# A new order on all engines in the first loop of a two-layer attention and experts kernel

## What is computed

```python
x = x + conv_attention(group_norm(x))     # q.k over a 3x3 neighbourhood, softmax, v, Wo
t = tokens(x)                             # 4 images x 4096 tokens x 256
n = layer_norm(t)
g = sigmoid(tanh(n @ Wp.T + bp) @ Wg.T)   # a gate per token
t = t + windowed_sum(g * n, 64) / windowed_sum(g, 64)
n = layer_norm(t)
p, e = top_2(softmax(n @ router.T))       # 8 experts, 2 for each token
t = t + sum_over_2(p * (gelu(n @ w1[e] + b1[e]) @ w2[e] + b2[e]))
```

## Time and profile before

| | us |
|---|---|
| median of 3 runs | 1681.78 (1677.89 to 1684.32) |
| the profiled execution | 1676.88 |
| its span, first to last instruction | 1674.9 |
| busy in the span: PE, DVE, ACT, POOL | 1308.2, 1143.7, 932.6, 858.6 |
| mean granted TensorE clock | 0.878 of full speed |

### The profile page before, as it was taken

One profiled execution on the slowest core, in us unless ns is written; L12 is line 12 of the kernel. 1 busy time (PEld: TensorE's weight loads), 2 busy tenths in 40 slices (PEclk: granted clock), 3 DMA queues, 4 the chain that ended last, 5 costly groups with the idle time before them and its releaser, 6 DMA issues. The chain is left out here.

```text
span 1674.9 us, 29587 instructions
## 1 busy us (share of the span) xinstructions
PE 1308.2 (78%) x8800; PEld 1156.5 (69%) x8800; DVE 1143.7 (68%) x3961; ACT 932.6 (56%) x2027; POOL 858.6 (51%) x864
## 2 busy tenths in 40 slices
PE   2289898999989998999987259999999999623232
PEld 2178787888877787788875249999999999522222
DVE  7447888888888788888884735656565656355554
ACT  1177576676666666676753246767677776311111
POOL 2234565667657566576654506666666666500000
PEclk7599999999999999999996569999999999855555
DMA  9445522223313123132211465555455544299997
GB/s 337 140 158 111 143 73 89 83 90 99 103 64 105 67 96 108 58 105 83 86 67 54 113 164 166 167 164 170 160 169 160 171 159 159 79 340 338 328 329 271
DMA packets 117819, 248.08 MB, mean 148 GB/s; under 512 B 40481, under 2 KB 54049, under 8 KB 113441
## 3 DMA queue, kind: packets, MB, share of 16 engines
q1 hardware_dynamic: 78624, 155.71, 30.1%
q0 software_dynamic: 26112, 71.60, 12.1%
q10 hardware_dynamic: 12928, 18.89, 3.2%
HBM read 132.57 MB, written 113.57 MB: 147 GB/s over the span
## 5 line engine op out<-in xcount | busy, mean ns | idle before, releaser
L1566 POOL DMA_INDIRECT answers<-yy,dest_i x288 | 302.9, 1052 | 194.6 <-DVE dest_i L1680 123.0
L1436 POOL DMA_INDIRECT sent<-tn,slot_s x256 | 256.2, 1001 | 171.1 <-DVE mix L1289 98.8
L1692 DVE TENSOR_TENSOR xl<-m_bank,xh 128x512 fp32r<-128x512 f32 x144 | 92.9, 686 | 179.2 <-ACT xh L1662 179.1
L1788 PE MATMUL m_bank<-ident,tot 128*128 128x128 f32 x256 | 63.0, 427 | 157.6 <-DVE tot L1773 157.6
L740 PE MATMUL o_bank<-vv,at 128*128 128x256 f32 x512 | 142.4, 402 | 43.5 <-ACT at L922 23.6
L1656 ACT ACTIVATE hid<-m_bank,b1s 128x512 f32<-128x512 f32 x144 | 98.9, 689 | 134.2 <-issue 87.5
L1615 PE MATMUL s_bank<-band,hh 128*128 x576 | 167.4, 291 | 0.9 <-DVE yy L1707 0.9
L1788 PEld LDWEIGHTS m_bank<-ident,tot 128*128 128x128 f32 x256 | 50.2, 223 | 170.2 <-DVE tot L1773 170.2
L1615 PE MATMUL s_bank<-w_s,hh 128*128 x576 | 160.8, 279 | 0.0
L1615 PE MATMUL s_bank<-band,hl 128*128 x576 | 160.6, 279 | 0.0
L1802 ACT ACTIVATE fin<-m_bank 128x512 f32<-128x512 f32 x64 | 38.1, 597 | 188.2 <-PE m_bank L1788 188.2
(11 more groups left out here) (214 smaller groups left out, 3890.4 us busy)
## 6 DMA issues: line engine op xcount, KB each, us to landing
xin<-sent SPq DMA_DIRECT2D x72, 516.0 KB, 3.8
got<-answers SPq DMA_DIRECT2D x32, 1024.0 KB, 7.1
xs<-in_x SPq DMA_DIRECT2D x32, 512.0 KB, 9.2
raw<-in_x SPq DMA_DIRECT2D x32, 512.0 KB, 3.7
residual<-tt SPq DMA_DIRECT2D x32, 512.0 KB, 4.5
res<-residual SPq DMA_DIRECT2D x32, 512.0 KB, 8.6
out_x<-fin ACTq DMA_DIRECT2D x32, 512.0 KB, 7.2
sent<-blank SPq DMA_DIRECT2D x12, 512.0 KB
```

Of the source, the lines that this page charges most:

```text
L1436: eng.indirect_dma_start(sent, bass.IndirectOffsetOnAxis(slot_s[:, par, j, k:k + 1], 0), tn[:, par, k, :], None).then_inc(scattered[par], 16)
L1566: eng.indirect_dma_start(answers, bass.IndirectOffsetOnAxis(dest_i[:, slot, k:k + 1], 0), yy[:, slot, k, :], None).then_inc(rows_out[slot] ...
L1692: eng.tensor_tensor(xl[:, par, c, :], xT_bank[c][:, :], xh[:, par, c, :].bitcast(f32), ALU.subtract).then_inc(xl_ready[c].sem, 1)
L1788: last = eng.transpose(m_bank[c][:, k * P:(k + 1) * P], tot[:, par, k, c * P:(c + 1) * P], ident[:, :])
```

## The change

In the first loop, all five engines get another order of the same pieces. No instruction is added or taken away.

- POOL: `band_lower` and `halo_rows` come first in a turn, then the two `power`, `summed`, and at the end the sends, now of stage S with lag 3 instead of 4: a block is sent in the turn in which its slots are made.
- DVE: `choices` goes from stage E to stage D of the same block, so from near the head of a turn to the middle of the turn before, behind `best_of` and `tokens(0)`. `aggregates(1)` goes from the end of a turn to the head of the next one, `mask(1)` to behind `mask(0)`, `query_part` behind `placed`, `tokens(3)` stays last, `edge_terms` goes behind `windowed(3)`, one `gated_part` behind the first `windowed`.
- PE: `positions` moves towards the head, the second `attend`, `weigh`, `values` and `window` change places, and `JOBS` with them, so the jobs meet other banks.
- ACT: `x_biased` moves from before the last `take_at` of a turn to the head of the turn that uses it; the value tiles, `take_at` and `band_upper` change places.
- SP: the load of new rows waits for the `x_biased` of this turn instead of the one before, which is the same block.

```diff
-LAG = {"N": -2, "A": -1, "V": -1, "B": 0, "C": 1, "D": 2, "E": 3, "S": 4}
+LAG = {"N": -2, "A": -1, "V": -1, "B": 0, "C": 1, "D": 2, "E": 3, "S": 3}
...
-        JOBS = ("BX01 VV0 AV1 AR0 AR1 Dtr01 Epos Dtr23 Ctr01 Ctr23 Drouter Cproj AV4 Cgate AV2 AV3 Cwin0 "
-                "Cwin1 Cwin2 BX23 Cwin3").split()
+        JOBS = ("BX01 Epos VV0 AV1 AR0 AR1 Dtr01 Dtr23 Ctr01 Ctr23 Drouter Cproj AV2 Cgate AV4 AV3 Cwin0 "
+                "Cwin1 BX23 Cwin2 Cwin3").split()
...
-        xb_ready = sig("xb_ready", "Axb")
+        xb_ready = sig("xb_ready", "Bxb")
...
-                        xb_ready.wait(eng, it.before(), "Axb")
+                        xb_ready.wait(eng, it, "Bxb")
                         load_rows(eng, two.block("N") + XROWS)
...
                 def positions(it):
 
-                    route.wait(eng, it, "EM")
+                    route.wait(eng, it.before(), "DM")
...
                 def choices(it):
-                    route.wait(eng, it.before(), "Dbesti")
-                    step(it, route, "Eidf", eng.tensor_copy(idf[:, :, :], besti[:, :, 0:2]))
+                    route.wait(eng, it, "Dbesti")
+                    step(it, route, "Didf", eng.tensor_copy(idf[:, :, :], besti[:, :, 0:2]))
...
                 def send(it, k0, k1):
                     par = it.parity("S")
                     if k0 == 0:
-                        alone(eng, (route.sem, route.count(it.before(), "Esl")))
+                        alone(eng, (route.sem, route.count(it, "Esl")))
...
                     n, a, c, d, s = (it.runs(x) for x in "NACDS")
-                    if s:
-                        send(it, 0, KT // 2)
-                        send(it, KT // 2, KT)
                     if a:
                         band_lower(it)
+                    if n:
+                        halo_rows(it)
                     if d:
                         power(it, 1)
                     if c:
                         power(it, 0)
                     if d:
                         summed(it)
-                    if n:
-                        halo_rows(it)
+                    if s:
+                        send(it, 0, KT // 2)
+                        send(it, KT // 2, KT)
```

More of the change, by code:

```diff
@@ L843, in body @@
                         logits(it, 1)
+                    if e:
+                        positions(it)
                     if a:
@@ L1004, in body @@
                     if b:
+                        x_biased(it)
                         x_taken(it, 0)
+                        expo(it, 0)
+                    if it.runs("V"):
+                        value_taken(it, 0)
+                    if a:
+                        value_taken(it, 1)
                     if e:
@@ L1104, in aggregates @@
                     else:
-                        alone(eng, (ln.sem, ln.count(it, "Cst2")))
+                        alone(eng, (ln.sem, ln.count(it.before(), "Cst2")))
                     for k in range(KT):
@@ L1295, in body @@
                         mask(it, 0)
+                        mask(it, 1)
+                    if d:
+                        aggregates(it, 1)
+                        variance(it, 1)
                     if c:
@@ L1321, in body @@
                     if b:
-                        mask(it, 2)
+                        sum_turned(it, 0)
                     if e:
-                        placed(it)
                         sending(it)
                     if b:
+                        mask(it, 2)
                         sum_turned(it, 1)
-                        tokens(it, 0)
                         mask(it, 3)
@@ L1335, in body @@
                     if b:
+                        tokens(it, 0)
                         sum_turned(it, 2)
+                    if d:
+                        choices(it)
                     if c:
@@ L1352, in body @@
                     if c:
+                        windowed(it, 1)
+                    if b:
+                        tokens(it, 2)
+                    if c:
                         gates_turned(it, 2)
-                        windowed(it, 1)
+                        windowed(it, 2)
+                        gates_turned(it, 3)
+                        windowed(it, 3)
                     if a:
@@ L1357, in body @@
                     if c:
-                        windowed(it, 2)
-                        gates_turned(it, 3)
-                    if b:
-                        tokens(it, 2)
-                    if c:
-                        windowed(it, 3)
-                    if b:
-                        sum_turned(it, 3)
-                    if c:
                         taken[bank_of["Cwin3"]].wait(eng, it, "Cwin3")
                         statistics(it, 1)
-                        aggregates(it, 1)
                     if b:
```

80 lines of the change are left out of this document (30 added, 50 removed).

## The result

The changed kernel takes 1743.74 us (1741.89 to 1744.40), the kernel before, on the same chip, 1679.84 (1677.27 to 1684.32). The ratio is 1.037, 95% interval 1.034 to 1.040: slower, by 64 us, against a forecast of 1736. The profiled execution has a span of 1742.1 us against 1674.9.

A forecast was written before the change was run, and what follows sets the result against it. PE was taken to bound the first loop, 25.7 us a turn. Turns of 23.4 + 3.1 (hold) + 1.3 (clock) = 27.8 gave +57, less 3 at the ends: 1731, plus 4.9 to the median, 1736 us; own range 1715 to 1765, 8-in-10 1632 to 1765.

The forecast's parts named there:

- (a): choices on DVE, moved beside the sends: loses its hold, 2.63 to about 0.65 us; PE's 0.80 us wait before positions goes.
- (b): x_biased on ACT, moved behind the last take_at: PE's 0.89 us wait before the last weigh goes.
- (c): attend(0) and weigh(0) side by side on PE: uncovered transposes and ACT copy cost 0.4 to 0.7 us, value 0.5.
- (d): Sends on POOL: start no sooner in its cycle, only halo_rows changes place; also the load on SP: 0.
- (e): DVE's head, mask 0 to the end of slot_s: from 10.4 to 7.9 to 8.2 us, so sends and band_lower come sooner.
- (f): DVE beside POOL's band_lower: line 1143 begins 0.3 us before it and is held, about 3.1 us reaching PE, repeating each turn.
- The clock's: PE's slower clock behind the wait for the held instruction: taken as 1.3 us a turn, bounded by 0 and 2.5.
- Rival 2: Larger lead: query_bias gets through, edge_terms is held 1 to 2 us, keeping the lead large; turn 24.2, 1642 us; chance 0.24.
- Rival 1: The lead is right, but PE's clock does not fall: turns of 26.5 us, 1700 us; chance 0.14.
- rival 3: No hold on DVE matters at all: 23.4 us in all turns, long ones gone, 1620 us; chance 0.10.
- rival 4: DVE held in about every second turn: 25.6 us a turn, within 8 us of no change; chance 0.10.
- Rival 5: The hold is one instruction long, DVE slipping in after band_lower's first half: turn 25.0, 1663 us; chance 0.04.

The follow-up runs named there:

- run 3: Kernel before, with only choices moved from stage E to stage D behind best_of, and positions waiting for the turn before: 1746.8 us, ratio 1.040.
- run 1: Changed kernel, with gated_part(3) moved ahead of the first gates_turned, and query_bias and edge_terms behind tokens(3) on DVE: 1623.2 us, ratio 0.966.
- run 6: Kernel before, with choices moved to stage D and query_bias and edge_terms behind tokens(3): 1634.2 us, ratio 0.971.
- run 8: Kernel of run 1, with attend(0) again behind queries(0), weigh(0) behind logits(2), take_at(0) ahead of main_rows: 1626.9 us, ratio 0.966.
- run 4: Changed kernel, with POOL's old order: sends one turn later again at the head of POOL's body, halo_rows last: 1738.1 us, ratio 1.034.
- run 7: Changed kernel, with 16 extra matmuls on PE ahead of window(3), in its wait for the held gated_part(3): 1706.8 us, ratio 1.014.
- run 5: Kernel before, with only query_bias and edge_terms moved behind tokens(3) on DVE: 1750.5 us, ratio 1.038.
- run 2: Changed kernel, with one added wait on POOL: band_lower waits until edge_terms of the turn before is done on DVE: 1643.7 us, ratio 0.978.

## Why the prediction was right

It forecast slower, 1736 us, by a hold that is repeated in nearly every turn, and got 1743.7 by that mechanism. Part of the nearness is luck. The terms gave +54 us on the profiled execution, and it was +67.2 (1676.88 to 1744.11): the 27 turns took 73.7 more, not 57, and the ends gave back 6.5, not 3. Then 4.9 us were added to get from the profiled execution to the median, and the changed kernel's profiled execution stands at its median (0.4 above), so this addition covered a part of what the terms were short. The stated range does not follow from its own terms either: by the formula, turns of 26.5 to 29.0 us give 1700 to 1768, not 1715 to 1765. The steps:

- Part (a) holds: the four instructions lost their hold, and the wait of 0.80 at `positions` went. Run 3 shows that it is also what starts the loss.
- Parts (b) and (c) were wrong in their sum: I had -0.9 and +0.5, a turn of 23.4. Both waits did what was said of them in the changed kernel, none at `weigh(3)` for ACT and 0.47 at `weigh(0)`, but the turn did not follow. The un-held turn is 23.80 with them and 23.80 without (runs 1 and 6). The gain of 0.8 us is (a)'s alone. The failed step is the sum of PE's gaps as if each were a price by itself: the 0.9 us stayed, at another place in each of runs 1, 6 and 8.
- Part (d): right. Run 4 undoes it, and the time (ratio 1.034 against 1.037) and the held instructions stay.
- Part (e): right. From mask 0 to the end of `slot_s` it is 634.38 to 642.55, 8.2 us; 7.9 to 8.2 were worked out.
- Part (f): the collision comes, but one instruction sooner than said. The 10.9 us from the slots to `band_lower` (642.55 to 653.43) stand as I had them, 11.03. I had line 1143 begin 1.2 us behind `windowed(0)` and `band_lower` 1.5. `band_lower` was 0.9 behind it (652.49 to 653.43), and `gated_part(3)`, which stands 0.5 behind it, was the one queued at that moment. This turned 22 of 27 holds into a wait of PE's window and not only of `tokens`. The four turns with `query_bias` held were as described, at 27.0 to 27.4 us (27.8 forecast).
- The hold's price of 3.1 us is 2.9 in run 7. The clock's, 1.3 with bounds of 0 and 2.5, was mis-sized: 1.9 in a usual turn, 1.7 in the mean of run 7's profile, 1.4 by the medians (the ratio falls by 2.2%, 38 us in 27 turns). I had taken 1.3 as about the middle of the bounds, without a row for it. With `gated_part` held PE waits twice within 3.8 us, 2.10 and then 0.97, and behind that its clock was at the lower level of 1.2 GHz, as in this stretch (PE alone, then clock and DMA):

```profile
659.00:663.00 4.00, 4.00 (x17) 0.50 0.34 129
```

  Two waits in place of one are not shown to be the reason. In the turn at 578.1 `query_bias` was held, PE waited once for `tokens`, 3.5 us, and the clock was 0.90; in the turn at 265.3 PE had the same 2.10 and 0.97, and it stayed at 1.00. What decides between the two is open.

```profile
578.10:605.50 27.40, 22.69 (x140) 19.75 (x139) 22.39 (x93) 17.24 (x40) 16.96 (x18) 0.90 0.28 96
265.30:293.90 28.60, 24.45 (x177) 21.55 (x176) 22.25 (x92) 17.91 (x41) 17.01 (x17) 1.00 0.24 80
```

- Added up, a usual turn is 23.8 + 2.9 + 1.9 = 28.6 against my 23.4 + 3.1 + 1.3 = 27.8: two terms short by 0.4 and 0.6, one long by 0.2.
- The ends of the loop: I took 3 us off, and 6.6 came off behind the last mask 0, in the emptying of the pipeline. Its first 26 us ran at a granted clock of 0.97 where the kernel before had 0.62 (first the change, then before):

```profile
943.80:970.00 26.20, 16.47 (x130) 13.59 (x128) 21.96 (x107) 10.73 (x29) 15.03 (x14) 0.97 0.17 62
```

```profile
870.00:896.20 26.20, 21.01 (x97) 16.65 (x96) 14.40 (x68) 10.04 (x25) 11.97 (x11) 0.62 0.17 61
```

From the last mask 0 to the end, the change and the eight runs other than run 5 took 791.1 to 798.3 us, the kernel before 804.9 and run 5 811.8. These are single profiled executions, and executions of the kernel before differ among themselves by up to 13 us (1675.8 to 1689.0). So it is not shown that the 6.6 us are the change's, nor what made them.

Rival 2 is seen once, in the turn at 552.2: `edge_terms` held for 2.68 us. It took 25.9 us, not 24.2, and the next turn was back at `query_bias`. The larger lead did not keep itself up, as that rival needed. Rival 1 fell with run 7, rivals 3 and 4 with the trace: 27 turns of 27 had a held instruction. Rival 5 said that DVE slips in behind the first half of `band_lower`. All of the full holds, 5 before, 26 in the change and 26 in run 3, ran to the end of both halves. The Trainium skill, page SBUF — State Buffer, section Who interferes with whom, says that whoever issues first has the shared ports for the whole instruction. The rows agree that it is an exclusion, and the DVE instructions with one operand in PSUM were free beside it (run 1); but here the holder was a pair of instructions. Line 1138 was held too, with one SBUF tile as input; whether that is the 2-port case that the prediction quotes from the same section, no run here shows.

## What to carry to other kernels

On an engine pair that excludes each other, the position of a long GpSimd instruction decides which DVE instruction of each turn pays, and a real gain upstream moves that position. Before freeing time ahead of a send or a long GpSimd piece, put what reads two SBUF tiles out of the new place, and then measure both edits together: here each alone was 4% slower, and the pair 3% faster (runs 3, 5, 6). Ask of a moved piece two questions, what it lies beside and what now stands behind it (run 5 failed on the second). Where PE is the busiest engine, price a stall at its length and then look at the clock behind it: waits of 2.1 and 1.0 us in a turn cost 1.7 more here, and filling the first of them with products that are thrown away was worth 2.2%. The best version here is the change with `gated_part(3)`, `query_bias` and `edge_terms` moved (run 1): 1623.2 us, ratio 0.966; run 8's 1626.9 is no different from it by the intervals.

## What was not expected of the hardware

- A DVE instruction can be held though it began before the GpSimd instruction's own recorded start. In the change, before and run 3, such instructions began up to 0.72 us ahead of `band_lower`. The prediction put the safe lead between 0.59 and 0.81 us; the runs narrow this. `gated_part(3)` was free at 0.72 and 0.73 ahead (the change, turns at 322.2 and 778.1) and at 0.71 (run 7), and line 1143 was held at 0.72 and free at 0.77 (run 3). So the border lies near 0.7 us and differs a little between the instructions. In run 2, where `band_lower` waits for the semaphore that `edge_terms` gives, line 1145 began 0.37 us ahead of it and took its normal 0.21. Whether what counts is that the instruction is queued and ready was not tried by itself.
- The clock's fall is not in proportion to the wait. PE's wait of 0.80 us in each turn kept the clock at 1.00 (24.6 us turns), and one of 1.84 at the same place brought 0.94 in the usual turn (run 5), with 1.6 us of slower work.
- One gap of 2.12 us between the first and second indirect DMA, in the same turn of the loop, in the kernel before, the change and all nine runs; `band_lower` comes later by it. What causes it was not looked for.
